# Cross attention and a routed feed-forward layer on one core: the hidden blocks of four tiles are written one place sooner in SyncE's queue, and the first vector steps change places

## The chip, the cores and the metric

The kernel runs on one core of one Trainium2 chip. The metric is the device time of one execution in microseconds (us), the median of several runs. The kernel before: 429.78 us, the median of 3 runs (424.73, 433.81 and 429.78).

## What is computed

The reference, cut to what matters. `x` is (8, 512, 512), 4096 rows of 512; the context is (8, 120, 512); there are 8 experts, each with two 512x512 matrices.

```python
x = x + xattn(k=ctx, v=ctx, q=layernorm(x), Wk, Wq, Wv, bv, bq, Wo, bo)   # softmax attention, one head
xf = layernorm(x).reshape(-1, 512)
idx = argmax(softmax(xf @ Wg + bg))                    # one expert for each row
h = gelu(xf @ W1[e] + b1[e])                           # exact gelu
y = h @ W2[e] + b2[e]
out = x + y[the row's expert]
```

## The kernel before

**Stages.** Up to about 95 us the weights are prepared and products that don't depend on `x` are made. Then 32 tiles of 128 rows go through the attention (about 95 to 205 us). Each row is normalised, its expert is picked, and GpSimd scatters it with an indirect transfer into a DRAM area `routed`, where every expert has its own span. Then the feed-forward part runs over NJ = 39 tiles of 128 routed rows, numbered 0 to 38, each with one expert.

**One tile t of the feed-forward part**, with the helpers that do it:

1. SyncE's queue loads the rows twice: `load_blocks(t)` (line 565, four transfers, as column blocks for the turn) and `load_rows(t)` (line 548, for the residual).
2. VectorE's `x2_turn(t)` (line 1220) transposes 32x32 blocks; ScalarE's `x2_high(t)` (line 946) and VectorE's `x2_low(t)` (line 1225) split the result into two float16 parts.
3. TensorE's `up(t)`: 12 matmuls (lines 1626 and 1629), the up-product, with results in one of two banks. It waits for `x2_low(t)` and for the copy of tile t-2.
4. ScalarE's `copy_hidden(t)` (line 954) copies the product out of the bank. SyncE's `write_hidden(t)` (line 575) writes it to a DRAM block, one for even and one for odd tiles, and `load_hidden(t)` (line 583) reads it back as column blocks, once the write has landed.
5. VectorE's `h_turn(t)` (line 1301) turns it, ScalarE's `gelu(t)` (line 960) and `g_high(t)` (line 968) and VectorE's `g_low(t)` (line 1306) follow.
6. TensorE's `down(t)`: for the first eight tiles one matmul that spreads the bias (line 1617) and then 12 matmuls. The bias matmul waits for `finish(t-2)`, which frees the bank, and the 12 wait for `g_low(t)`.
7. GpSimd's `residual(t)` (line 766, with 774 for tiles from 8 on) prepares the residual, VectorE's `finish(t)` (line 1312) adds the product, and GpSimd's `send(t)` (line 780) scatters the rows to the output.

**Order on TensorE around the change**: up 0, up 1, up 2, up 3, up 4, down 0, the count of the tiles, down 1, and from there up t followed by down t-3: up 5, down 2, up 6, down 3, up 7, down 4, up 8, down 5, up 9 and so on. Between them stand eight single matmuls that spread biases (line 1617 too).

**Tables.** Which rows and which expert a tile has stands in a table. Its first eight columns (NE = 8) are made early from the first rows counted. The other 31 come from lines 1345 to 1372 on VectorE (the *late table*), after all rows are counted, and each reader waits for it. SyncE then loads first rows into registers (line 539, one load of so many values).

**Queues.** Every engine works through its own list in order, and a waiting instruction holds up all behind it. On SyncE `step(t)` runs in the order `write_hidden(t)`, `load_blocks(t+4)`, `load_rows(t+3)`, `load_hidden(t)`. Exceptions at the start: `load_blocks(5)` follows `load_hidden(0)`. In step 5 (`NE - 3`) the order is `write_hidden(5)`, `load_hidden(5)`, the wait for the late table and all scattered rows, one load of seven values, `load_blocks(8)`, `load_blocks(9)`, `load_rows(8)`. On VectorE `step(t)` runs `finish(t-4)`, `g_low(t-2)`, `h_turn(t-1)`, `x2_low(t+2)`, `x2_turn(t+3)`, with the first of these written out by hand. GpSimd scatters the last four row tiles (line 743), then makes the residuals 0 to 2.

## Time and profile before

| | value |
|---|---|
| runs shown | 424.73, 433.81, 429.78 us, median 429.78 |
| the profiled execution | 431.77 us, of which the span from first to last instruction is 430.0 us |
| busy in the span | TensorE 397.0 us, VectorE 321.3, GpSimd 261.1, ScalarE 251.1 |

How to read it: busy time is an average over stages. TensorE is busy for 92% of the span, so time can only come out of its pauses and out of stretches in which it runs at half its clock. In the rows below, the timeline has the start in us, the duration in us, the engine, the line, the operation, what it writes and reads, how many instructions are merged, and in brackets how long the engine had stood idle and what ended that.

### The profile page before, as it was taken

To read this page: it belongs to the slowest core of one execution; us is meant where nothing else is said; L and a number is where in the kernel's file an instruction comes from. 1 tells how busy PE (TensorE), PEld (TensorE's weight loads), DVE (VectorE), ACT (ScalarE), POOL (GpSimd) and SP (SyncE) were. 2 spreads that over 40 slices of the span, in tenths; PEclk is the share of its full clock that TensorE was granted. 3 is DMA by queue.
4 is the path that set the end of the run, shared out by engine and by line. 5 is a ranking of instruction groups with operands and counts; after the bars stand their busy time and mean duration, and the time that the engine had idled before them with its cause. 6 is when DMAs were issued, how large, how long until landed. Compare 5 with 4: busy or idle time off the path is not lost.

```text
span 430.0 us, 8879 instructions
## 1 busy us (share of the span) xinstructions
PE 397.0 (92%) x2097; PEld 219.8 (51%) x2097; DVE 321.3 (75%) x658; ACT 251.1 (58%) x571; POOL 261.1 (61%) x338
## 2 busy tenths in 40 slices
PE   7999999979999998978879799999999999999980
PEld 4657774648777676653334244444444444444430
DVE  4399939994688788887787587778868896988640
ACT  5351128668888887855565365555555555656530
POOL 6089861409457877676783347668546776576730
PEclk9999999999999999998999899999999999999996
DMA  8998999908345596464895887988798979898510
GB/s 274 375 390 297 341 423 416 361 6 319 99 164 176 159 329 183 154 206 129 258 279 164 225 247 235 254 238 225 228 267 249 264 247 258 233 270 240 182 51 0
DMA packets 77984, 101.19 MB, mean 235 GB/s; under 512 B 9075, under 2 KB 49023, under 8 KB 76152
## 3 DMA queue, kind: packets, MB, share of 16 engines
q1 hardware_dynamic: 69664, 80.74, 61.1%
q0 software_dynamic: 6400, 19.65, 12.4%
q10 hardware_dynamic: 1880, 0.31, 0.4%
q8 instruction: 19, 0.31, 0.3%
q14 instruction: 21, 0.17, 0.1%
HBM read 70.80 MB, written 31.28 MB: 237 GB/s over the span
## 4 chain that ended last, share of the span: by engine, by line
PE 41%; DMA 19%; DVE 11%; SPq 11%; issue 9%; POOL 5%; ACT 2%; DVEq 0%; ACTq 0%; POOLq 0%
PE bank L1626 9%; DMA hidden_blocks<-work 7%; DMA work<-hidden_blocks 6%; SPq L565 5%; PE bank L1533 5%; PE bank L1629 5%; PE bank L1468 5%; POOL routed_rows L743 3%; DMA hidden_blocks<-keys_values_then_rows_b 3%; PE bank L1409 3%; PE bank L1488 2%; DMA routed_rows<-work,slot_index 2%; PE bank L1564 2%; PE bank L1580 2%; PE bank L1448 2%
## 5 line engine op out<-in xcount | busy, mean ns | idle before, releaser
L780 POOL DMA_INDIRECT out_x<-keys_values_then_rows_b x39 | 42.5, 1089 | 62.9 <-DVE keys_values_then_rows_b L1312 57.3
L1626 PE MATMUL bank<-expert_weights 128*128 x312 | 75.4, 385 | 4.5 <-DVE expert_weights L1225 2.8
L1626 PE MATMUL bank<-expert_weights,ey_bias_split_then_geluT 128*128 x312 | 74.7, 383 | 3.7 <-DVE ey_bias_split_then_geluT L1306 3.7
L960 ACT ACTIVATE work<-work,b_columns 128x128 f32<-128x128 f32 x144 | 46.0, 390 | 20.6 <-DVE work L1301 15.6
L1301 DVE STREAM_TRANSPOSE work<-work 128x512 f32<-128x512 f32 x36 | 41.4, 1150 | 20.5 <-DMA work<-hidden_blocks 20.4
L1626 PEld LDWEIGHTS bank<-expert_weights 128*128 128x128 f16 x312 | 30.8, 99 | 44.0 <-issue 12.2
L954 ACT ACTIVATE work<-bank 128x512 f32<-128x512 f32 x36 | 21.5, 596 | 53.6 <-PE bank L1629 53.5
L1626 PEld LDWEIGHTS bank<-expert_weights,ey_bias_split_then_geluT 128*128 128x128 f16 x312 | 30.6, 98 | 41.1 <-issue 7.5
L774 POOL TENSOR_TENSOR keys_values_then_rows_b<-keys_values_then_rows_b 128x512 f32<-128x512 f32 x31 | 43.1, 1390 | 7.7 <-POOL keys_values_then_rows_b L766 7.5
L743 POOL DMA_INDIRECT routed_rows<-work,slot_index x32 | 33.1, 1035 | 23.6 <-DVE slot_index L1169 15.6
L1629 PE MATMUL bank<-expert_weights,ey_bias_split_then_geluT 128*128 x156 | 40.8, 385 | 0.0
L766 POOL TENSOR_SCALAR keys_values_then_rows_b<-keys_values_then_rows_b 128x512 f32<-128x512 f32 x39 | 35.8, 920 | 8.0 <-ACT keys_values_then_rows_b L974 6.2
L1629 PE MATMUL bank<-expert_weights 128*128 x156 | 40.2, 380 | 0.0
L1306 DVE TENSOR_TENSOR ey_bias_split_then_geluT<-work,ey_bias_split_then_geluT 128x512 f16<-128x512 f32 x36 | 26.8, 743 | 13.3 <-ACT ey_bias_split_then_geluT L968 13.1
L825 ACT ACTIVATE expert_weights<-expert_weights 128x512 f16<-128x512 f32 x52 | 31.7, 625 | 8.2 <-DVE expert_weights L1082 8.1
L1082 DVE SCALAR_TENSOR_TENSOR expert_weights<-expert_weights 128x512 f16<-128x512 f32 x52 | 34.8, 700 | 1.4 <-ACT expert_weights L825 0.4
L1580 PE MATMUL bank<-keys_values_then_rows_b,work 120*128 120x512 f32 x64 | 35.3, 634 | 0.0
L1564 PE MATMUL bank<-keys_values_then_rows_b,work 128*128 128x128 f32 x256 | 33.8, 275 | 0.0
L1225 DVE TENSOR_TENSOR expert_weights<-key_bias_then_xn,expert_weights 128x512 f16<-128x512 f32 x39 | 32.3, 829 | 1.4 <-ACT expert_weights L946 1.4
L1564 PEld LDWEIGHTS bank<-keys_values_then_rows_b,work 128*128 128x128 f32 x256 | 31.1, 192 | 0.6 <-ACT work L891 0.6
L946 ACT ACTIVATE expert_weights<-key_bias_then_xn 128x512 f16<-128x512 f32 x39 | 24.2, 619 | 11.4 <-DVE key_bias_then_xn L1220 11.1
L1312 DVE SCALAR_TENSOR_TENSOR keys_values_then_rows_b<-bank,keys_values_then_rows_b 128x512 f32<-128x512 f32 x39 | 25.6, 656 | 4.3 <-PE bank L1629 4.2
(214 smaller groups left out, 749.3 us busy)
## 6 DMA issues: line engine op xcount, KB each, us to landing
expert_weights<-in_L_ffn_W SPq DMA_DIRECT2D x14, 1024.0 KB, 14.4
keys_values_then_rows_b<-routed_rows SPq DMA_DIRECT2D x39, 258.0 KB, 3.6
hidden_blocks<-work SPq DMA_DIRECT2D x36, 256.0 KB, 3.8
work<-hidden_blocks SPq DMA_DIRECT2D x36, 256.0 KB, 3.4
expert_weights<-in_x SPq DMA_DIRECT2D x16, 512.0 KB, 4.8
expert_weights<-in_x SPq DMA_DIRECT2D x24, 256.0 KB, 3.2
work<-routed_rows SPq DMA_DIRECT2D x72, 64.0 KB
key_bias_then_xn<-routed_rows SPq DMA_DIRECT2D x68, 64.0 KB, 2.7
```

Source lines behind the costliest of these rows:

```text
L743: pool.indirect_dma_start(routed, bass.IndirectOffsetOnAxis(ap=slot_i[:, j:j + 1], axis=0), rows[:, j, :], None).then_inc(sent[j], 16)
L766: x1_again = nc.gpsimd.tensor_scalar(row[:, 0:D], row[:, 0:D], row[:, D + 3:D + 4], row[:, D:D + 1], ALU.mult, ALU.add)
L774: nc.gpsimd.tensor_tensor(row[:, 0:D], row[:, 0:D], kv[:, bass.ds(ex + b2_at, D)], ALU.add).then_inc(res_ready, 1)
L780: pool.indirect_dma_start(out_rows, ids_of, rrow[t.buf][:, 0:D], None, bounds_check=T - 1, oob_is_err=False).then_inc(out_sent[t.buf], 16)
L960: nc.scalar.activation(hid_turned_of(t)[:, P * c:P * (c + 1)], hid_turned_of(t)[:, P * c:P * (c + 1)], ACT.Gelu, bias=b1_cols[:, :, :].rea ...
L1082: nc.vector.scalar_tensor_tensor(w_split[:, bass.ds(n * 2 * D + D, D)], wall[:, bass.ds((n + GAP) * D, D)], WSCALE, w_split[:, bass.ds(n * ...
L1225: nc.vector.tensor_tensor(x2T[t.half][:, C:2 * C, :], xn2_turned.rearrange("p (c t) -> p c t", c=C), x2T[t.half][:, 0:C, :], ALU.subtract) ...
L1301: nc.vector.transpose(hid_turned_of(t).rearrange("p (c j a) -> p a c j", c=C, a=C), hid_in_of(t).rearrange("p (a i c) -> p a c i", a=C, c= ...
L1564: mm(bank[2 + j % 2][:, 0:P], xnT[j % 2][:, c, :], kv[:, bass.ds(b * (2 * D) + c * P, P)], start=(c == 0), stop=False)
L1580: mm(bank[6 + j % 2][:, :], probT[j % 2], kv[0:K, bass.ds(b * (2 * D) + D, D)], start=True, stop=True)\
L1626: mm(o, a[:, c, :], w_split[:, bass.ds(first + (2 * c + h) * D, D)], start=(c == 0 and h == 0 and not begun), stop=False)
L1629: last = mm(o, a[:, C + c, :], w_split[:, bass.ds(first + 2 * c * D, D)], start=False, stop=(c == C - 1))
```

## The change

On SyncE:

- `write_hidden(1)` to `write_hidden(4)` move ahead in the queue: 1 stands behind `load_hidden(0)` and ahead of `load_blocks(5)`; 2 ahead of `load_hidden(1)`; 3 ahead of `load_hidden(2)`; 4 ahead of `load_hidden(3)`, which now also stands ahead of `load_blocks(7)` and `load_rows(6)`.
- Each `write_hidden` outside the loop waits besides until the block's earlier contents were read (`hl_in`): tile 2 for `load_hidden(0)`, 3 for 1, 4 for 2, and so on.
- In step 5 the late table is read in two parts: one value, `load_blocks(8)`, then `load_hidden(5)`, then six values, then `load_blocks(9)`.

On ScalarE `copy_hidden(3)` goes ahead of `gelu(0)`, and `copy_hidden(4)` ahead of `gelu(1)`. On VectorE `h_turn(1)` goes ahead of `g_low(0)`; `finish(0)`, `g_low(2)`, `h_turn(3)` and `finish(1)` go ahead of the late table, `g_low(3)` into it ahead of its first comparison; `h_turn(4)` and `x2_low(7)` follow `x2_turn(7)`; and `x2_turn(8)` goes behind `finish(2)` and `g_low(4)`. On GpSimd `residual(0)` and `residual(1)` go ahead of the wait for the last picks. No product, copy, turn or byte moved by a transfer is added or taken away.

```diff
             def write_hidden(t):
                 wait_apart(sp, hc_done, t.j + 1, sp_waits)
+                if isinstance(t.j, int):
+                    need(sp, hl_in[t.half], 16 * t.pair)
                 sp.dma_start(hidden[...], hid_of(t)...).then_inc(hw_in[t.half], 16)
...
             def step(t):
-                if t.real:
+                if t.real and not (isinstance(t.j, int) and 0 < t.j <= C):
                     write_hidden(t)
+                if isinstance(t.j, int) and t.j == C - 1:
+                    write_hidden(t + 1)
+                    load_hidden(t)
                 if isinstance(t.j, int) and t.j == NE - 3:
+                    late_ready()
+                    starts.update(enumerate(first_rows(NE, 1), NE))
+                    load_blocks(t + 3, starts[(t + 3).base])
                     load_hidden(t)
-                    late_ready()
-                    starts.update(enumerate(first_rows(NE, FIRST + 4 - NE), NE))
-                    load_blocks(t + 3, starts[(t + 3).base])
+                    starts.update(enumerate(first_rows(NE + 1, FIRST + 3 - NE), NE + 1))
...
+                if isinstance(t.j, int) and t.j in (1, C - 2):
+                    write_hidden(t + 1)
-                if t.real and not (isinstance(t.j, int) and t.j == NE - 3):
+                if t.real and not (isinstance(t.j, int) and t.j in (C - 1, NE - 3)):
                     load_hidden(t)
                 if isinstance(t.j, int) and t.j == 0:
+                    write_hidden(Slot(1))
                     load_blocks(Slot(C + 1), starts[C + 1])
...
# GpSimd, scale()
                 if n == 2 * NTURN - 1:
+                    residual(Slot(0))
+                    residual(Slot(1))
                     pool.wait_ge(picked, n + 1)
...
-            for n in range(3):
-                residual(Slot(n))
+            residual(Slot(2))
...
# ScalarE
-                if t.real:
+                if t.real and not (isinstance(t.j, int) and t.j <= C):
                     copy_hidden(t)
...
+            copy_hidden(Slot(3))
             gelu(Slot(0))
             g_high(Slot(0))
+            copy_hidden(Slot(4))
...
# VectorE
             pick_experts(c, 2 * NTURN - 1, 1)
+            h_turn(Slot(1))
             g_low(Slot(0))
-            h_turn(Slot(1))
             place(c, 2 * NTURN - 1, 1)
...
             h_turn(Slot(2))
+            finish(Slot(0))
             x2_low(Slot(5))
             x2_turn(Slot(6))
+            g_low(Slot(2))
+            h_turn(Slot(3))
+            finish(Slot(1))

             dve.wait_ge(counted, 1)
...
-            g_low(Slot(2))
-            finish(Slot(0))
             x2_low(Slot(6))
+            g_low(Slot(3))
...
-            h_turn(Slot(3))
...
             x2_turn(Slot(7))
+            h_turn(Slot(4))
+            x2_low(Slot(7))
...
                 if (t - 2).real:
                     g_low(t - 2)
+                if isinstance(t.j, int) and t.j == NE - 2:
+                    x2_turn(t + 2)
...
-            each_step(dve, step, 5, NJ + 4)
+            each_step(dve, step, NE - 2, NJ + 4)
```

## Rows read from the trace of the kernel before

**Rows 1.** Windows: stretch, PE, PEld, DVE, ACT, POOL busy, clock, DMA share, GB/s

```profile
242.00:244.00 2.00, 2.00 (x6) 0.69 (x5) 1.87 (x3) 1.97 (x6) 1.17 (x1) 0.50 1.10 297
262.00:320.00 58.00, 57.84 (x268) 26.09 (x267) 45.81 (x54) 33.01 (x77) 37.85 (x34) 1.00 0.85 246
```

**Rows 2.** Waits, 205 to 246 us: total us, times, longest

```profile
PE bank L1617 <- DVE keys_values_then_rows_b L1312: 4.3, 2, 2.5
```

**Rows 3.** Timeline of TensorE, down 1 to up 9

```profile
218.43 1.90 PE L1626 MATMUL bank<-expert_weights,ey_bias_split_then_geluT 128*128 x8 [1.11 <-DVE ey_bias_split_then_geluT L1306]
...
226.11 0.39 PE L1617 MATMUL bank<-b_split,expert_rows_one_hot 104*128 104x512 f16 x1 [1.86 <-DVE keys_values_then_rows_b L1312]
...
240.21 0.39 PE L1617 MATMUL bank<-b_split,expert_rows_one_hot 104*128 104x512 f16 x1 [2.47 <-DVE keys_values_then_rows_b L1312]
240.81 2.89 PE L1626 MATMUL bank<-expert_weights,ey_bias_split_then_geluT 128*128 x8 [0.22 <-DVE ey_bias_split_then_geluT L1306]
...
245.09 1.89 PE L1626 MATMUL bank<-expert_weights 128*128 x8
...
251.15 1.89 PE L1626 MATMUL bank<-expert_weights 128*128 x8
```

**Rows 4.** Timeline of SyncE's queue, tiles 1 to 9 of the feed-forward part

```profile
206.78 0.46 SPq L575 DMA_DIRECT2D hidden_blocks<-keys_values_then_rows_b  x1
...
211.52 0.34 SPq L583 DMA_DIRECT2D keys_values_then_rows_b<-hidden_blocks  x1
...
219.94 0.41 SPq L583 DMA_DIRECT2D keys_values_then_rows_b<-hidden_blocks  x1
220.41 0.45 SPq L575 DMA_DIRECT2D hidden_blocks<-work  x1
...
232.59 0.32 SPq L583 DMA_DIRECT2D keys_values_then_rows_b<-hidden_blocks  x1
235.02 1.89 SPq L565 DMA_DIRECT2D work<-routed_rows  x4
...
239.43 0.42 SPq L575 DMA_DIRECT2D hidden_blocks<-work  x1
...
242.77 0.35 SPq L583 DMA_DIRECT2D work<-hidden_blocks  x1
```

**Rows 5.** Issue to landing of the hidden blocks 184 to 262 us: line 575, then line 583

```profile
DMA to landing us min/median/max: 3.1/3.9/6.8
...
DMA to landing us min/median/max: 2.8/3.6/5.9
```

**Rows 6.** Table loads of 7 values and of 1

```profile
L539 SPq TENSOR_LOAD <-tile_table x1: 1625/1625/1625, 233.2 to 233.2; - x1
...
L539 SPq TENSOR_LOAD <-tile_table x1: 280/280/280, 392.8 to 392.8; - x1
```

**Rows 7.** Timeline of VectorE, 209 to 249 us

```profile
213.18 1.00 DVE L1306 TENSOR_TENSOR ey_bias_split_then_geluT<-work,ey_bias_split_then_geluT 128x512 f16<-128x512 f32 x1 [1.16 <-ACT ey_bias_split_then_geluT L968]
...
221.98 0.13 DVE L1345 SCALAR_TENSOR_TENSOR tiles_int<-bank,expert_base_rows 128x8 int32<-128x8 f32 x1
...
229.39 0.33 DVE L1369 TENSOR_SCALAR tile_table<-late_table_by_column 1x31 int32<-1x31 f32 x3
...
238.41 1.08 DVE L1220 STREAM_TRANSPOSE key_bias_then_xn<-work 128x512 f32<-128x512 f32 x1 [4.63 <-DMA work<-routed_rows]
...
247.25 1.13 DVE L1301 STREAM_TRANSPOSE work<-work 128x512 f32<-128x512 f32 x1 [2.31 <-DMA work<-hidden_blocks]
248.27 0.65 DVE L1225 TENSOR_TENSOR expert_weights<-key_bias_then_xn,expert_weights 128x512 f16<-128x512 f32 x1
```

**Rows 8.** Timeline of ScalarE, copy 3

```profile
213.05 0.58 ACT L954 ACTIVATE keys_values_then_rows_b<-bank 128x512 f32<-128x512 f32 x1
```

**Rows 9.** Timeline of GpSimd at the wait for the last picks

```profile
212.12 3.45 POOL L735 TENSOR_SCALAR work<-work,neg_mean_x 128x512 f32<-128x512 f32 x4 [2.03 <-DVE expert_one_hot L1154]
```

**Rows 10.** Line 766 on GpSimd, 222.5 to 225 us: ns min/median/max

```profile
L766 POOL TENSOR_SCALAR keys_values_then_rows_b<-keys_values_then_rows_b x4: 761/797/1225, 222.5 to 224.8; 128x512 f32<-128x512 f32 x4
```

## The prediction

> **What bounds the kernel now.** I read first the busy time by windows, then TensorE's waits, then the timelines of TensorE, SyncE's queue and VectorE side by side. From 262 to 320 us TensorE is busy for 57.84 of 58 us at full clock [rows 1]; the reader is to see that in the steady part nothing but TensorE's own work counts, and that a start made earlier by some us brings the end forward by as much, if the rest keeps up. What can be won lies between the first down-products and up 9. There TensorE waited 4.3 us in two places for `finish`, which frees the bank of the down-product [rows 2]. In order of time [rows 3]: 1.11 us at down 1, 1.86 at the bias matmul of down 2, 2.47 and 0.22 at down 4. Then down 4 ran at half clock (0.50, its level of 1.2 GHz [rows 1]): its 12 matmuls take from 240.81 to 245.09, 4.3 us, where a product takes 2.6 (up 9 of rows 3 stands 6.06 after up 8, which is two products, 5.2, and the bias matmuls between). That costs 1.7. Together 1.11 + 1.86 + 2.47 + 0.22 + 1.7 = 7.4 us.
>
> What stands behind the 2.47 us is on VectorE: `x2_turn(8)` waited 4.63 us for its column blocks, with `finish(2)` and `g_low(4)` behind it [rows 7]. Its transfers left SyncE's queue only at 235.02, while the late table was ready at 229.7 (229.39 + 0.33) [rows 4, 7]: the queue stood at `load_hidden(5)`, issued at 232.59, and then loaded seven values in 1.62 us [rows 4, 6].
>
> **SyncE, the writes.** No transfer is added. `write_hidden(1)`, 206.78 before, no longer has the four transfers of `load_blocks(5)` ahead (four take 1.89 us [rows 4]): 204.8. Tile 2's write follows about 208.3 (after the four block transfers, a row load and the landing of `load_hidden(0)`), `load_hidden(1)` about 209.5 instead of 211.52. `copy_hidden(3)`, 213.05 before, loses `gelu(0)` and `g_high(0)` ahead of it and comes as soon as up 3 is done, about 2 us sooner [rows 8]. Tile 3's write waits (new) for `load_hidden(1)`: 209.5 + 3.6 [rows 5], 213. `load_hidden(2)` leaves at 213.4 and lands at 217.0, and the second new wait, that of `write_hidden(4)`, is over only then. Queued behind that wait are `load_hidden(3)`, `load_blocks(7)`, two row loads and `load_hidden(4)`. Still `write_hidden(4)` leaves at 217.1 instead of 220.41 and `load_hidden(3)` at 217.5 instead of 219.94 [rows 4]. From there landings are slow, since the last four scatters are on the DMA engines: the longest write took 6.8 us and the longest read 5.9, where the medians are 3.9 and 3.6 [rows 5]. For `load_hidden(3)` the bounds are 2.8 and 5.9 (6.8 if it fares like the write); I take 5.9, since that is what this very transfer is the likeliest to meet: landed at 223.4.
>
> **VectorE.** `h_turn(1)` ahead of `g_low(0)` waits for `load_hidden(1)`, about 213, and takes 1.1, so `g_low(0)`, which ran at 213.18 [rows 7], starts about 0.4 later, and down 0 with it: cost 0.4. `gelu(1)` starts sooner for it, and down 1 comes at 217.6 with 0.1 us of waiting instead of 1.11. Down 2's bias matmul no longer waits, as `finish(0)` comes ahead of the table's work, and down 2 is over at 226.1. But `h_turn(3)` now stands ahead of the table, and waits for `load_hidden(3)` until 223.4. From the first table instruction to the last the work before took 229.72 - 221.98 = 7.7 us [rows 7], with a turn, a `finish`, an `x2_low` and a `g_low` among it. The new order from `h_turn(3)` on has the same four and the same table work, so the table is ready at 223.4 + 7.7 = 231.1, 1.4 later than before. Halfway, 4.9 after `h_turn(3)` begins (7.7 less the half of the table, 2.1, and a `g_low`, 0.7: my estimate), `x2_low(6)` is done at 228.3, and TensorE waits for it at up 6: 228.3 - 226.1 = 2.2 us. That is what is late next.
>
> **SyncE, the table.** One value takes 0.28 us and seven 1.62 [rows 6], so six take about 1.40 ((1.62 - 0.28) / 6 = 0.22 each): one and six together cost the same as seven, plus some 0.3 us around a load. `load_blocks(8)` leaves at 231.1 + 0.28 + 0.5 = 231.9, 3.1 sooner than 235.02. Then come `load_hidden(5)`, 233.8 (1.2 later than 232.59, hidden: its turn stands behind `x2_turn(8)` and down 5 isn't due before 243), six values and `load_blocks(9)` and `load_rows(8)`: `write_hidden(6)` leaves at about 238.8 instead of 239.43; the queue sets this, not tile 6's copy, which is ready some us before. `load_hidden(6)` leaves at 242.1 instead of 242.77.
>
> **TensorE at up 9.** `finish(2)` and `g_low(4)` no longer stand behind `x2_turn(8)`: down 4 starts at about 237 without a long wait, 3.7 sooner, and at full clock. Up 8 follows at 240 and down 5 is over at 246.3. Up 9 needs `x2_low(9)`, which VectorE does behind `h_turn(6)`. Before, `h_turn(6)` waited 2.31 us for `load_hidden(6)`, and `x2_low(9)` ended at 248.92 [rows 7], 2.2 us ahead of up 9 at 251.15 [rows 3]. Now it ends 0.7 sooner, 248.2, and up 9 waits 1.9 us for it. The sum: 7.4 removed, 0.4 + 0.1 + 2.2 + 1.9 = 4.6 new, net 2.8 us; the direct reading agrees, up 9 at 248.3 instead of 251.15. From there TensorE has nothing but its own work again, since `write_hidden` and `load_hidden` need less than its 5.2 us a tile (0.4, four block transfers 1.9, 0.4, 0.35 and the rest of a landing).
>
> **GpSimd.** `residual(0)` and `residual(1)` fill the 2.03 us that it waited for the last picks [rows 9]; two take 2 x 0.8 = 1.6 us, and 2.4 at the slow end of line 766 [rows 10]. If the cover were gone the scatters would go 0.4 later. I cost it at nothing. In rows 10 the same instruction takes 761 ns and 1225 ns, so something beside it holds it up. The Trainium skill (SBUF — State Buffer, Who interferes with whom) says that VectorE instructions with two SBUF inputs and GpSimd instructions that read SBUF lock each other out for a whole instruction. By that rule VectorE's picks, which now run beside a residual, could lose up to one residual; the sum would then be 2.0 and not 2.8.
>
> **The time.** The profiled execution took 431.77 us with a span of 430.0. 430.0 - 2.8 = 427.2, execution 429.0, a ratio of 0.9935; on the median of 429.78 that is 427.0.
>
> **Rivals.**
> (a) *Forecast*: 427.0, with 426 to 428.5 as its own range. For it: `load_hidden(6)` hangs on the queue behind the table, which moves little.
> (b) *The gain is given back at up 6 and up 9.* The waits of 2.2 and 1.9 us are about as long as the 2.47 us after which the clock fell before. If it falls at one, 1.7 us go; at both, 3.4. Against: after the 1.86 us at down 2 it didn't fall. Time 428.7 to 430.4.
> (c) *Landings at their fast end.* If `load_hidden(3)` and those before it take 2.8 to 3.1 us [rows 5], each hand-over moves up: `load_hidden(3)` lands at 217.6, `h_turn(3)` then waits only for VectorE's own order and starts at 220.6, the table is ready at 228.3, `load_hidden(6)` leaves at 239, up 9 starts at 244. Net 7.2, time 422.6. For: the writes leave ahead of the scatters. Against: `load_hidden(3)` doesn't. The Trainium skill (DMA: Bandwidth & Descriptors, Anatomy of one DMA) gives about 2 us fixed plus bytes over 436 GB/s, an estimate of 2.6 us for these 256 KB, and by that this rival would hold; the trace has 2.8 as its shortest, 5.9 and 6.8 as its longest.
> (d) *Slower: the new wait of `write_hidden(4)` dams the queue.* Place: step 3 of SyncE. If `load_hidden(2)` lands at 219 and `load_hidden(3)` at 227, the table comes at 234.7, and up 9, 17.2 us behind the table (248.3 - 231.1), at 251.9: time 430.5; with both at 6.8 us after queueing, 432. It decides from a landing of `load_hidden(3)` at 226.2, 2.8 later than I take.
> (e) *The change does nothing*, as the medians hide it: the three runs differ by 9 us.
>
> **Chances.** (a) 0.42, (b) 0.25, (c) 0.18, (d) 0.15; (e) lies within the first two. The prediction is (a), 427.0. The range of 421.5 to 431.5 takes in (c) with 1 us beyond, and (d) up to 431.5; it is as wide as this since the runs themselves spread by 4 to 5 us about their median. 2% of 429.78 is 8.6 us, about what a measurement here can tell from no change: only (c) with a median of luckier runs reaches below 421.2, 0.08, and only (d) with unlucky ones above 438.4, 0.04. Within 2%: 0.88.
>
> **What the profile after would show.** Right: no wait of TensorE for line 1312; down 4 at clock 1.00; `x2_turn(8)` behind line 1306 with less than 1 us of waiting; a wait of about 2 us for line 1225 at up 6 and at up 9; late table at 231; `load_blocks(8)` 3 us sooner. Wrong: line 583 of tile 3 landed by 221 or after 226, the clock at 0.50 after either wait, or new waits for line 1306 in the steady part, which would mean that the chain through SyncE doesn't keep up.

## The result, and the profile after

The changed kernel takes 432.25 us (median of 20 runs, 428.03 to 438.28), the kernel before 430.15 us (20 runs, 424.73 to 435.68): ratio 1.0068, 95% interval 1.0046 to 1.009. On another chip the ratio was 1.0129 (1.0078 to 1.018). A ratio is taken over the runs within 1.5% of their kernel's fastest, so it isn't quite the quotient of the medians. The change makes the kernel slower by 0.7 to 1.3%, 3 to 5.5 us.

Two traces were taken of each kernel. Three marks of TensorE's timeline cut them: the start of up 4, the start of up 9 and the end of the span. The last column is the sum of TensorE's waits for `x2_low` from 255 to 400 us.

| trace | span | up 4 starts | up 4 to up 9 | up 9 to the end | waits for `x2_low`, 255 to 400 us |
|---|---|---|---|---|---|
| before | 430.0 | 210.27 | 40.9 | 178.9 | 0.6 |
| before, second | 422.9 | 206.56 | 38.4 | 178.0 | 0.2 |
| after | 431.6 | 208.50 | 40.5 | 182.6 | 3.4 |
| after, second | 432.2 | 209.85 | 39.1 | 183.3 | 4.3 |

Up to up 9 the two kernels are alike (39.6 us on average before, 39.8 after). The loss stands behind it: 4.5 us, from 178.4 to 182.9 on average, in a part whose code was not touched. By TensorE's busy time in that part (165.0 and 164.6 us before, 165.9 twice after), about 3.5 of the 4.5 us are idle time and about 1 is longer busy time, which no run explains.

TensorE's timeline of the changed kernel, the lines that answer to [rows 3] (columns as there; up and down are lines 1644 and 1647, `g_low` is 1318, `x2_low` 1237, `h_turn` 1313, `x2_turn` 1232, `finish` 1324):

```profile
216.19 3.59 PE L1644 MATMUL bank<-expert_weights,ey_bias_split_then_geluT 128*128 x8 [4.59 <-DVE ey_bias_split_then_geluT L1318]
...
221.28 0.21 PE L1723 MATMUL bank<-picks_seen,ones_f 128*128 128x8 f16 x1
...
249.01 1.90 PE L1644 MATMUL bank<-expert_weights 128*128 x8 [1.06 <-DVE expert_weights L1237]
...
266.22 1.90 PE L1644 MATMUL bank<-expert_weights 128*128 x8 [1.03 <-DVE expert_weights L1237]
...
277.25 1.90 PE L1644 MATMUL bank<-expert_weights 128*128 x8 [0.50 <-DVE expert_weights L1237]
...
288.28 1.90 PE L1644 MATMUL bank<-expert_weights 128*128 x8 [0.50 <-DVE expert_weights L1237]
```

The waits for `finish` of [rows 2] are gone, as forecast. In their place, down 0 waited 4.59 us for `g_low(0)` and then took 5.1 us (216.19 to 221.28) where a product takes 2.6. And there are waits for `x2_low` in the steady part, at a distance of 11.03 us from each other, which is two tiles. The windows of the changed kernel answer to [rows 1]: half clock at down 0, and in the steady part TensorE busy 55.38 of 58 us instead of 57.84 (a few records are missing from either):

```profile
218.00:220.00 2.00, 2.00 (x6) 0.63 (x5) 1.54 (x2) 0.92 (x3) 1.39 (x3) 0.50 0.56 189
...
262.00:320.00 58.00, 55.38 (x254) 24.74 (x253) 47.45 (x52) 31.92 (x73) 36.84 (x33) 1.00 0.82 239
```

SyncE's queue of the changed kernel (line 577 writes a hidden block, 585 loads it; compare [rows 4]), and what ended the waits on ScalarE and VectorE:

```profile
204.67 0.45 SPq L577 DMA_DIRECT2D hidden_blocks<-keys_values_then_rows_b  x1
...
210.15 0.34 SPq L585 DMA_DIRECT2D keys_values_then_rows_b<-hidden_blocks  x1
...
218.70 0.51 SPq L585 DMA_DIRECT2D keys_values_then_rows_b<-hidden_blocks  x1
...
233.73 1.87 SPq L565 DMA_DIRECT2D work<-routed_rows  x4
...
240.02 0.40 SPq L577 DMA_DIRECT2D hidden_blocks<-work  x1
...
243.27 0.35 SPq L585 DMA_DIRECT2D work<-hidden_blocks  x1
```

```profile
210.16 0.60 ACT L964 ACTIVATE keys_values_then_rows_b<-bank 128x512 f32<-128x512 f32 x1 [2.72 <-DMA hidden_blocks<-keys_values_then_rows_b]
211.11 1.28 ACT L970 ACTIVATE work<-work,b_columns 128x128 f32<-128x128 f32 x4 [0.35 <-issue]
...
227.20 0.60 ACT L964 ACTIVATE keys_values_then_rows_b<-bank 128x512 f32<-128x512 f32 x1 [2.44 <-PE bank L1647]
227.69 1.08 ACT L984 ACTIVATE keys_values_then_rows_b<-bank 128x512 f32<-128x512 f32 x2
228.65 1.28 ACT L970 ACTIVATE keys_values_then_rows_b<-keys_values_then_rows_b,b_columns 128x128 f32<-128x128 f32 x4
```

```profile
214.39 1.13 DVE L1313 STREAM_TRANSPOSE keys_values_then_rows_b<-keys_values_then_rows_b 128x512 f32<-128x512 f32 x1 [3.58 <-DMA keys_values_then_rows_b<-hidden_blocks]
215.39 0.66 DVE L1318 TENSOR_TENSOR ey_bias_split_then_geluT<-work,ey_bias_split_then_geluT 128x512 f16<-128x512 f32 x1
...
230.62 0.69 DVE L1318 TENSOR_TENSOR ey_bias_split_then_geluT<-keys_values_then_rows_b,ey_bias_split_then_geluT 128x512 f16<-128x512 f32 x1 [2.16 <-ACT ey_bias_split_then_geluT L978]
...
232.91 0.33 DVE L1383 TENSOR_SCALAR tile_table<-late_table_by_column 1x31 int32<-1x31 f32 x3
```

The reader is to see three things. Write 1 left at 204.67, 2.1 us sooner than in [rows 4], but was in DRAM only at 210.1, after 5.4 us, and its reading, issued at 210.15, landed at 214.4, after 4.2 us. `h_turn(1)` stood idle 3.58 us for it, with `g_low(0)` behind it, whose input had been ready since 213.0: down 0 waited for a turn that it doesn't need. And the late table was ready at 233.2, since `g_low(3)`, now in the middle of it, waited 2.16 us for `gelu(3)` and `g_high(3)` (line 978). The turn was not what it lacked: `h_turn(3)` had ended at 225.8. But on ScalarE `gelu(3)` (228.65) stands behind `copy_hidden(5)` (227.20) and two copies of biases (line 984), and `copy_hidden(5)` had waited 2.44 us for up 5, which came late by what down 0 had lost. In the same way `copy_hidden(3)`, put ahead of `gelu(0)`, waited 2.72 us for write 1 to land (210.16), and `gelu(0)` began at 211.11, 1.2 us behind the end of `h_turn(0)` (209.87), where it had been 0.1 before.

### The profile page after: what moved, and what is told of

Its sections match the earlier page's. It is cut to its first block, busy times and chain, and to the rows that moved or that the text cites. A ratio compares the mean times of both kernels' runs of the same rounds, so it can differ in the third digit from the quotient of the medians.

```text
span 431.6 us, 8893 instructions
## 1 busy us (share of the span) xinstructions
PE 397.3 (92%) x2097; PEld 219.1 (51%) x2097; DVE 323.1 (75%) x658; ACT 251.9 (58%) x571; POOL 260.4 (60%) x338
## 4 chain that ended last, share of the span: by engine, by line
PE 45%; DMA 14%; issue 12%; DVE 11%; SPq 8%; POOL 4%; ACT 3%; another core or an unknown queue 0%; ACTq 0%; POOLq 0%; DVEq 0%
PE bank L1644 10%; DMA work<-hidden_blocks 6%; PE bank L1551 5%; PE bank L1647 5%; PE bank L1486 5%; SPq L565 5%; PE bank L1582 4%; PE bank L1427 3%; PE bank L1598 3%; PE bank L1506 2%; DMA hidden_blocks<-work 2%; PE bank L1574 2%; DVE expert_weights L1237 2%; POOL routed_rows L754 2%; DMA routed_rows<-work,slot_index 2%
## 5 line engine op out<-in xcount | busy, mean ns | idle before, releaser
L791 POOL DMA_INDIRECT out_x<-keys_values_then_rows_b x39 | 40.7, 1043 | 66.2 <-DVE keys_values_then_rows_b L1324 59.5
L1644 PE MATMUL bank<-expert_weights 128*128 x312 | 73.9, 379 | 6.9 <-DVE expert_weights L1237 5.7
L777 POOL TENSOR_SCALAR keys_values_then_rows_b<-keys_values_then_rows_b 128x512 f32<-128x512 f32 x39 | 37.7, 970 | 7.9 <-ACT keys_values_then_rows_b L984 6.1
L1647 PE MATMUL bank<-expert_weights,ey_bias_split_then_geluT 128*128 x156 | 40.9, 386 | 0.0
L1647 PE MATMUL bank<-expert_weights 128*128 x156 | 40.0, 379 | 0.0
L1237 DVE TENSOR_TENSOR expert_weights<-key_bias_then_xn,expert_weights 128x512 f16<-128x512 f32 x39 | 35.2, 902 | 1.4 <-issue 0.7
```

What stands on the lines that cost most here:

```text
L777: x1_again = nc.gpsimd.tensor_scalar(row[:, 0:D], row[:, 0:D], row[:, D + 3:D + 4], row[:, D:D + 1], ALU.mult, ALU.add)
L791: pool.indirect_dma_start(out_rows, ids_of, rrow[t.buf][:, 0:D], None, bounds_check=T - 1, oob_is_err=False).then_inc(out_sent[t.buf], 16)
L1237: nc.vector.tensor_tensor(x2T[t.half][:, C:2 * C, :], xn2_turned.rearrange("p (c t) -> p c t", c=C), x2T[t.half][:, 0:C, :], ALU.subtract) ...
L1644: mm(o, a[:, c, :], w_split[:, bass.ds(first + (2 * c + h) * D, D)], start=(c == 0 and h == 0 and not begun), stop=False)
L1647: last = mm(o, a[:, C + c, :], w_split[:, bass.ds(first + 2 * c * D, D)], start=False, stop=(c == C - 1))
```

## The experiments

Two theories at the start. T1: the loss is down 0 (the wait and the half clock). T2: it arises behind up 9. Each kernel below is timed against the kernel before on its own chip; ratios carry a 95% interval. "Gap" is up 4 to up 9 and "rest" is up 9 to the end, in us, from one trace.

**e1: `g_low(0)` first.** The changed kernel with one pair put back.

```diff
             pick_experts(c, 2 * NTURN - 1, 1)
-            h_turn(Slot(1))
             g_low(Slot(0))
+            h_turn(Slot(1))
```

> The changed kernel with one line of VectorE's list put back: g_low(0) ahead of h_turn(1). Theory T1 (the loss comes from down 0, which waited 4.59 us behind h_turn(1) and then ran at half clock, 2.5 us): down 0 waits about 1 us as before and runs at clock 1.00, up 9 starts 3 to 6 us sooner after up 4 than the 40.5 us of the changed kernel, and the time is 3 us or more below the changed kernel's, ratio to before 0.99 to 1.00. Theory T2 (the loss arises behind up 9, in the steady part: 182.6 us from up 9 to the end against 178.9 before): what is won ahead of up 9 does not reach the end, the stretch from up 9 to the end stays at 182 us or grows, ratio to before 1.004 to 1.01.

Measured: ratio 1.0012 (0.9974 to 1.005), 428.35 us. Gap 37.9, rest 181.3; the wait at down 0 is 2.00 us and the half clock is still there, where T1 expected 1 us and full clock (`copy_hidden(3)` holds `gelu(0)` back by 1.1 us in this trace too), and TensorE waits 1.37 us at 262.53 for `x2_low`. Against the changed kernel's 1.0068 and 1.0129 the one pair is worth 2.4 to 5 us, from ratios on different chips whose intervals allow 0.5 to 7.8; its gap is 1.9 us shorter than the changed kernel's average. But what the front wins over before (39.6 to 37.9) is given back in the rest (178.4 to 181.3). Both theories have a part.

**e2, e3, e4: one side of the change at a time.** e2 is the kernel before with the new SyncE and ScalarE, e3 with the new VectorE and GpSimd, e4 with the table in two parts and `x2_turn(8)` moved, nothing else:

```diff
                 if isinstance(t.j, int) and t.j == NE - 3:
+                    late_ready()
+                    starts.update(enumerate(first_rows(NE, 1), NE))
+                    load_blocks(t + 3, starts[(t + 3).base])
                     load_hidden(t)
-                    late_ready()
-                    starts.update(enumerate(first_rows(NE, FIRST + 4 - NE), NE))
-                    load_blocks(t + 3, starts[(t + 3).base])
+                    starts.update(enumerate(first_rows(NE + 1, FIRST + 3 - NE), NE + 1))
...
                     g_low(t - 2)
+                if isinstance(t.j, int) and t.j == NE - 2:
+                    x2_turn(t + 2)
...
-                if (t + 3).real:
+                if (t + 3).real and not (isinstance(t.j, int) and t.j == NE - 3):
                     x2_turn(t + 3)
```

> The kernel before with the new order of SyncE's queue and ScalarE's two copies, VectorE and GpSimd as before. T1: down 0 as before (wait about 1 us), so no loss; the writes come 2 to 3 us sooner but finish and x2_turn(8) still stand where they did; ratio 0.99 to 1.00. T2, if the queue's new phase makes the steady part slow: up 9 to the end 182 us instead of 178.9, ratio 1.004 to 1.01.

> The kernel before with VectorE's and GpSimd's new order, SyncE and ScalarE as before. h_turn(1) ahead of g_low(0) now waits for load_hidden(1) at its old place (landed about 214.3), so down 0 waits at least as long as in the changed kernel, 4.5 us or more. T1: slower than the changed kernel or equal to it, ratio to before 1.005 to 1.015, all of the loss standing ahead of up 9. T2: the stretch from up 9 to the end is 182 us in spite of SyncE's old order if VectorE's order is what changes the steady part, 179 if it is the queue's.

> The kernel before with two things only: the table read in two parts with load_blocks(8) ahead of load_hidden(5), and x2_turn(8) behind finish(2) and g_low(4). The prediction's reading of the 2.47 us at down 4: that wait and the half clock behind it (1.7 us) go, up 9 starts up to 2.2 us sooner. T1: this reaches the end, ratio 0.993 to 0.998. T2: up 9 to the end grows by as much, ratio 0.998 to 1.005.

Measured: e2 1.001 (0.9969 to 1.0051), e3 1.0028 (0.9992 to 1.0064), e4 0.9999 (0.996 to 1.0037). Gap and rest: e2 37.5 and 181.5; e3 40.1 and 179.7; e4 39.9 and 181.0. In e4 no wait of TensorE at down 4 is left. None of the three is measurably faster or slower than before, so e3 misses the 1.005 to 1.015 that T1 gave it. Each of the traces has waits for `x2_low` in the rest (2 to 4 us), which the two traces of before have not: either any of the moves calls them up, or two traces of before don't show all that it does. In e3 down 0 waited 4.54 us, with SyncE's old order: the long wait at down 0 comes with VectorE's order. But e2, with VectorE's old order, waited 2.52 us there, 0.9 more than the 1.65 of the second trace of before: in e2 `copy_hidden(3)` waited 1.78 us for write 1, with `gelu(0)` behind it.

**Before and after again.** No edit.

> The kernel before once more, one look, for a second trace. Where up 9 comes about 40.9 us behind up 4, the stretch from up 9 to the end is expected at 179 us with under 3 us of waits, as in the first trace. If it comes out at 181 or more, the first trace of before was lucky there and the comparison of the two steady parts from single traces doesn't hold.

> The changed kernel once more, for its ratio on the same chip as the next two and a second trace. Expected of both theories: ratio to before about 1.007, down 0 waits over 4 us and starts at half clock. T1 (h_turn(1) ahead of g_low(0) is the loss) expects it 2 to 3 us above the kernel with that line put back. If the trace's stretch from up 9 to the end is again about 182 us, the steady part is slower whenever up 9 is not late; if it is 179, the first trace had bad luck there.

Measured: the rest is 178.0 in the second trace of before and 183.3 in the second of after (ratio 1.0129), so in two traces of each the steady part is slower in the changed kernel. The second trace of before shows something else, in the same places as [rows 3]:

```profile
223.96 0.39 PE L1617 MATMUL bank<-b_split,expert_rows_one_hot 104*128 104x512 f16 x1 [1.75 <-DVE keys_values_then_rows_b L1312]
236.27 1.90 PE L1626 MATMUL bank<-expert_weights,ey_bias_split_then_geluT 128*128 x8 [0.21 <-DVE ey_bias_split_then_geluT L1306]
```

```profile
222.00:240.00 18.00, 15.95 (x73) 7.07 (x73) 15.36 (x32) 11.54 (x26) 8.14 (x8) 1.00 0.79 224
```

The wait of 2.47 us at down 4 and the half clock behind it are not there: 0.21 us, and a clock of 1.00. The traces of e7 and e12 (below), whose order is that of the kernel before up to down 4, haven't them either (no wait, and some 0.3 us), so they were a matter of one execution in four. A stretch at half clock is there all the same, at down 0, behind a wait of 1.65 us:

```profile
213.00:215.00 2.00, 2.00 (x6) 0.76 (x5) 1.79 (x6) 1.51 (x5) 0.97 (x3) 0.50 0.93 214
```

**What makes the steady part slow.** The chain of one round in the changed kernel: VectorE, SyncE, what SyncE's queue waited for from 255 to 400 us (line 78 is the helper in which it waits; total us, times, longest), and the instruction of GpSimd (line 785, the second of a residual) that ran beside the first `x2_low`:

```profile
263.19 1.15 DVE L1313 STREAM_TRANSPOSE work<-work 128x512 f32<-128x512 f32 x1 [2.45 <-DMA work<-hidden_blocks]
264.22 1.75 DVE L1237 TENSOR_TENSOR expert_weights<-key_bias_then_xn,expert_weights 128x512 f16<-128x512 f32 x1
266.11 1.10 DVE L1232 STREAM_TRANSPOSE key_bias_then_xn<-key_bias_then_xn 128x512 f32<-128x512 f32 x1
...
274.66 1.16 DVE L1313 STREAM_TRANSPOSE work<-work 128x512 f32<-128x512 f32 x1 [1.56 <-DMA work<-hidden_blocks]
275.70 1.30 DVE L1237 TENSOR_TENSOR expert_weights<-key_bias_then_xn,expert_weights 128x512 f16<-128x512 f32 x1
277.14 1.11 DVE L1232 STREAM_TRANSPOSE key_bias_then_xn<-key_bias_then_xn 128x512 f32<-128x512 f32 x1
```

```profile
267.44 1.86 SPq L565 DMA_DIRECT2D key_bias_then_xn<-routed_rows  x4
270.00 0.31 SPq L548 DMA_DIRECT2D keys_values_then_rows_b<-routed_rows  x1
270.69 0.35 SPq L585 DMA_DIRECT2D work<-hidden_blocks  x1
...
SPq L78 <- DVE key_bias_then_xn L1232: 18.1, 16, 2.1
```

```profile
264.15 1.27 POOL L785 TENSOR_TENSOR keys_values_then_rows_b<-keys_values_then_rows_b 128x512 f32<-128x512 f32 x1 [0.28 <-POOL keys_values_then_rows_b L777]
```

Read as one chain: `h_turn` starts at 263.19 as its block lands; `x2_low` behind it takes 1.75 us and frees up 12, which starts at 266.22 after a wait of 1.03; `x2_turn` ends at 267.2; that frees `load_blocks` on SyncE (267.44), behind which stand `load_rows` (270.00) and `load_hidden` (270.69); it lands at 274.6, and `h_turn` starts at 274.66. The way round is 11.5 us here and 10.9 the next time (`h_turn` at 285.56), TensorE's wait comes back at 277.25 and 288.28 (11.03), and two tiles of TensorE's work are 10.4 (four products of 2.6). It is a ring over two tiles with more in it, in these rounds, than TensorE's own time; from 290 to 400 us only two more waits follow, at 304.70 and 347.47, so it isn't too long in every round. Theory R says that this ring limits, L that GpSimd lengthens `x2_low` in it, P that an uneven start keeps it going, S1 that it is enough to take `x2_low` out of its shadow.

**e12: one delay in the kernel before.**

```diff
+                if isinstance(t.j, int) and t.j == NE - 1:
+                    for _ in range(14):
+                        link(nc.vector.memset(early_v[:, :], 0.0))
                 if (t - 1).real:
                     h_turn(t - 1)
```

> The kernel before with 14 small memsets in a chain on VectorE, some 2.5 to 3 us, once, ahead of h_turn(6). Theory P (one uneven start persists: in the changed kernels h_turn(6) stood idle 2.4 to 3.4 us and the waits for x2_low behind up 9 sum to 2.3 to 4.3 us): waits for x2_low up at up 9 and again every second tile up to about 300 us, 2 us or more behind up 9, time 1 to 3 us above before. If the pipeline forgets it, TensorE waits once at up 9, 1 us or less, and never again; ratio 1.000 to 1.003.

Measured: ratio 1.0032 (1.0002 to 1.0062), rest 180.6. The delay, and TensorE's waits from 255 to 400 us (total, times, longest), first of e12 and then of before for comparison:

```profile
243.29 2.83 DVE L1380 MEMSET early_table_scratch<- 128x80 f32 x14
...
PE bank L1629 <- DVE expert_weights L1225: 2.4, 5, 0.6
```

```profile
PE bank L1626 <- DVE expert_weights L1225: 0.6, 1, 0.6
```

TensorE lost some 0.3 us at up 9, yet five waits came later, the first at 275.28 and the next 11.03 behind it. That agrees with P, in one trace and with a ratio just clear of 1, but doesn't show it. The delay itself is smaller than the chain of 2.83 us, since VectorE stood idle at the same place in both traces of before (2.31 us [rows 7] and 1.37): `load_hidden(6)` left at 240.72, and with the 4.2 to 4.5 us that it took in these two it would have let `h_turn(6)` start at 244.9 to 245.2, not 246.16, an estimate of about 1 us.

What the delay changed can be read at up 9:

```profile
247.19 0.65 DVE L1225 TENSOR_TENSOR expert_weights<-key_bias_then_xn,expert_weights 128x512 f16<-128x512 f32 x1
...
248.09 1.90 PE L1629 MATMUL bank<-expert_weights 128*128 x8
```

Up 9 started 0.25 us behind the end of `x2_low(9)`, as soon as it could: in the changed kernel, where it waited, it is 0.24. Twelve traces have `h_turn` ahead of `x2_low` in the steps: in ten it is 0.24 or 0.25, and in the two of before `x2_low(9)` was ready 2.2 and 1.4 us ahead of up 9. So before enters the steady part with a reserve, and the others without one. That fits the waits that follow; that it causes them was not tested by itself.

**e13 and e14: what is in the ring.** e13 is the changed kernel with `load_rows(t+3)` behind `load_hidden(t)` from step 6 on. e14 is the changed kernel, and e9 is e1, each without the second instruction of a residual (line 785) for tiles from 8 on, so that the expert's bias is missing from their output.

```diff
-                if (t + 3).real and not (isinstance(t.j, int) and t.j < -1):
+                late = not isinstance(t.j, int) or t.j >= NE - 2
+                if (t + 3).real and not late and not (isinstance(t.j, int) and t.j < -1):
                     load_rows(t + 3, starts[(t + 3).base])
...
                     load_hidden(t)
+                if (t + 3).real and late:
+                    load_rows(t + 3, starts[(t + 3).base])
```

> The changed kernel with load_rows(t+3) behind load_hidden(t) in SyncE's steps from 6 on, so that one issue of 0.35 us and the gap before it leave the way from x2_turn through load_blocks to load_hidden. Theory R (a ring of two tiles: load_hidden lands, h_turn, x2_low, x2_turn, load_blocks, load_rows, load_hidden; 11.03 us a round in the changed kernel where TensorE needs 10.4): the round shortens by 0.35 to 0.8 us, TensorE's waits for x2_low behind 255 us fall from 3.4 and 4.3 us to under 2, ratio to before 1.000 to 1.006 instead of 1.0068 and 1.0129. If the queue is no part of the ring (only the hidden block's own round through DRAM counts), waits and time stay.

> The changed kernel without GpSimd's second instruction of a residual (the expert's bias is not added for tiles from 8 on, so that part of the output is left out). Theory L (GpSimd's instruction lengthens x2_low, which feeds the ring): x2_low's mean falls from 988 and 904 ns to 750 or less, TensorE's waits for it from 3.4 and 4.3 us to 1 to 2, the time by 2 to 4 us, ratio to before 0.995 to 1.003. If only the uneven start counts, x2_low gets short and the waits stay at 3 us or more.

> The changed kernel with g_low(0) first, without GpSimd's second instruction of a residual (the expert's bias is not added for tiles from 8 on, so that part of the output is left out). Theory L (GpSimd's residuals hold x2_low up: it takes up to 1.75 us instead of 0.65): x2_low falls to 0.65 to 0.8 us each, TensorE's waits for it in the steady part shrink by half or more, and the time falls by 1 to 3 us. If x2_low gets short and the waits stay, they come from the hidden block's landing alone.

Measured: e13 1.0063 (1.001 to 1.0117), rest 181.0; e14 0.9981 (0.994 to 1.0021), rest 179.4; e9 0.9918 (0.9881 to 0.9956), rest 178.0. TensorE's waits from 255 to 400 us, of after, e13 and e14:

```profile
PE bank L1644 <- DVE expert_weights L1237: 3.4, 5, 1.0
```

```profile
PE bank L1647 <- DVE expert_weights L1240: 1.3, 3, 0.5
```

```profile
PE bank L1637 <- DVE expert_weights L1230: 1.0, 3, 0.6
```

`x2_low` from 250 to 400 us (28 or 29 times; busy us and mean ns), of before, after and e14:

```profile
L1225 DVE TENSOR_TENSOR expert_weights<-key_bias_then_xn,expert_weights 128x512 f16<-128x512 f32 x28 | 24.1, 862 | 0.0
```

```profile
L1237 DVE TENSOR_TENSOR expert_weights<-key_bias_then_xn,expert_weights 128x512 f16<-128x512 f32 x28 | 27.7, 988 | 0.0
```

```profile
L1230 DVE TENSOR_TENSOR expert_weights<-key_bias_then_xn,expert_weights 128x512 f16<-128x512 f32 x29 | 20.9, 721 | 0.0
```

Without GpSimd's instruction `x2_low` takes 721 ns instead of 988 and the waits for it fall from 3.4 to 1.0 us (in e9 740 ns, and 1.2 us instead of e1's 2.5): L holds. The mean alone doesn't tell the kernels apart, though: e4 has 3.6 us of waits with a mean of 863 ns, before 0.6 with 862. By the rule of the Trainium skill (SBUF — State Buffer, Who interferes with whom) `x2_low`, with two SBUF inputs, and GpSimd's instructions that read SBUF hold each other up for a whole instruction; the trace agrees: the `x2_low` of 264.22 took 1.75 us instead of 0.65 and ended at 265.97, 0.55 behind the end of the instruction of line 785 (264.15 + 1.27); at 275.70 and 286.59 it is 0.55 us again. For R the trace of e13 speaks (1.3 us of waits for `x2_low` and 0.4 without a releaser, under the 2 expected); its time doesn't decide, since the interval holds the changed kernel's 1.0068 as well as what R expected.

**e6, e7, e11: `x2_low` ahead of the turn.** The same edit on e1, on before and on the changed kernel, for every step:

```diff
-                if (t - 1).real:
-                    h_turn(t - 1)
                 if (t + 2).real:
                     x2_low(t + 2)
+                if (t - 1).real:
+                    h_turn(t - 1)
```

> The changed kernel with g_low(0) first, and besides, in each of VectorE's steps, x2_low(t+2) ahead of h_turn(t-1). Theory S1 (the steady part gives the gain back because x2_low stands behind an h_turn that waits for its hidden block): TensorE's waits for x2_low between 250 and 300 us (1.37 us at tile 12 in the kernel with g_low(0) first) go, up 9 to the end falls from 181.3 to about 178, ratio to before 0.990 to 0.995. Theory S2 (the chain write, read, turn, gelu, down is itself too long, so a wait only changes its name): TensorE waits as long for line g_low instead, and the time stays at 0.999.

> The kernel before with one thing only: in VectorE's steps x2_low(t+2) ahead of h_turn(t-1). Two traces of before have only 0.6 and 0.2 us of waiting for x2_low behind up 9, so if the order of the first tiles is worth what e6 showed over before, this one stays at 0.995 to 1.000, above e6 (0.990). If x2_low ahead of the turn is the whole of e6's gain, it comes out at 0.990 as well, and the change's own moves are worth nothing.

> The changed kernel (h_turn(1) still ahead of g_low(0)) with x2_low(t+2) ahead of h_turn(t-1) in VectorE's steps. If the loss has two terms, the one at down 0 stays (a wait of over 4 us and half clock) and the one in the steady part goes: up 9 to the end 177 to 178 us instead of 182.6 and 183.3, time 3 to 5 us below the changed kernel, ratio to before 0.997 to 1.002, and 2 to 3 us above e6. If the steady part stays slow, x2_low's place is not its cause.

Measured: e6 0.9899 (0.9846 to 0.9953), gap 36.1, rest 177.0; e7 0.992 (0.9882 to 0.9958), gap 40.6, rest 178.2; e11 0.9938 (0.9907 to 0.9968), gap 37.5, rest 177.0. No wait for `x2_low` is named behind 255 us in any of them (e7 has one wait of 0.98 us without a releaser). The window of e6 that answers to [rows 1]:

```profile
262.00:320.00 58.00, 58.00 (x271) 26.25 (x270) 43.97 (x57) 33.70 (x79) 38.95 (x35) 1.00 0.87 249
```

On the changed kernel the edit is worth 5.9 us of the rest by the traces (182.9 to 177.0), and its ratio falls from 1.0068 and 1.0129 to 0.9938: S1 holds, for the edit as a whole. It does two things at once, though: in its three kernels `x2_low` stands ahead of the wait for the hidden block, and it also takes only 722, 719 and 724 ns on average from 250 to 400 us (e6, e7, e11), as little as in e14, since it now runs at another time than GpSimd's instruction. By single traces the shorter `x2_low` alone (e14) brings the rest from 182.9 to 179.4, and the edit to 177.0. These three beat the kernel before by 0.6 to 1.0%, and the changed kernel by more. Among themselves they can't be told apart (e11, expected at 0.997 to 1.002, came out better), so the change's own moves (e7 has none of them, e11 all) are worth nothing that can be measured even where the steady part doesn't eat them. e11 keeps its 3.54 us of waiting at down 0 and isn't measurably slower than e7; against e6, from which it differs by the pair of e1 alone, it is 0.4% slower, 1.7 us, within the intervals.

**e10: `x2_turn` ahead of the turn too.** e6 with the last two of each step exchanged.

```diff
                 if (t + 2).real:
                     x2_low(t + 2)
-                if (t - 1).real:
-                    h_turn(t - 1)
                 if (t + 3).real:
                     x2_turn(t + 3)
+                if (t - 1).real:
+                    h_turn(t - 1)
```

> e6 with x2_turn(t+3) ahead of h_turn(t-1) too, so that SyncE's load_blocks, which waits for x2_turn, no longer hangs on the landing of a hidden block. If the loop of two tiles (load_hidden, h_turn, x2_turn, load_blocks, load_hidden) still limits anything in e6, the time falls 1 us or more, 0.986 to 0.989. If e6 is at TensorE's own rate from up 9 on (its stretch to the end was 177.0 us with 2 us of waits, all in the tail), it stays at 0.990, or rises by 1 us since the turn comes 1.1 us later and gelu with it.

Measured: ratio 1.0449 (1.04 to 1.0498), 448.79 us. I had expected 1 us at most either way from e6; it is 19 us above before, and some 23 above e6 by the ratios. VectorE's round, and what TensorE waited for from 255 to 400 us:

```profile
294.71 1.00 DVE L1318 TENSOR_TENSOR ey_bias_split_then_geluT<-work,ey_bias_split_then_geluT 128x512 f16<-128x512 f32 x1 [1.55 <-issue]
295.63 0.68 DVE L1237 TENSOR_TENSOR expert_weights<-key_bias_then_xn,expert_weights 128x512 f16<-128x512 f32 x1
296.45 1.11 DVE L1232 STREAM_TRANSPOSE key_bias_then_xn<-key_bias_then_xn 128x512 f32<-128x512 f32 x1
297.49 1.09 DVE L1313 STREAM_TRANSPOSE work<-work 128x512 f32<-128x512 f32 x1
...
PE bank L1644 <- DVE ey_bias_split_then_geluT L1318: 13.0, 22, 0.7
```

Here a ring of one tile closes: `g_low` 294.71, `x2_low`, `x2_turn`, `h_turn` to 298.6, then on ScalarE `gelu` (1.28) and `g_high` (0.63), and the next `g_low` at 300.68: 5.97 us a tile against TensorE's 5.2. In e6 `x2_turn`'s 1.1 us are outside this ring, and it needs 4.9 (an estimate, 5.97 less 1.1).

## Why the prediction was wrong

1. **"Together ... 7.4 us" can be won.** The sum of pauses was taken from one execution. Its largest term, 2.47 + 1.7 us at down 4, was absent from the second trace of before (0.21 us, clock 1.00) and from e7 and e12. Of the terms only the wait at down 2 stands in all four traces with this order (1.86, 1.75, 1.91 and 1.91 us); the 1.11 us at down 1 were 0, 1.00 and 0.21 in the other three, and the half clock was elsewhere. e4, which takes just the wait at down 4 away, measures 0.9999.
2. **"down 0 with it: cost 0.4".** `g_low(0)` came at 215.39 instead of 213.18, 2.2 us later. I took 3.9 and 3.6 us for the landings of write and read of tile 1, the medians of [rows 5], where 5.4 and 4.2 came. Besides, TensorE was 1.8 us earlier at that point than in the trace of before (up 4 at 208.50 instead of 210.27, which no edit brought), so the same lateness was a longer wait: 4.59 us. I had priced half clock at up 6 and up 9, but not here, where it fell: 2.5 us (5.1 less 2.6). That part isn't the change's alone, since the second trace of before, e7 and e12 have half clock at down 0 too. In the first pair of traces this step took 3.6 + 2.5 = 6.1 us instead of 0.4, which with 1.06 us at up 9 used up nearly all of the 7.4: up 4 to up 9 is 0.4 us shorter, not 2.8. `copy_hidden(3)` failed beside it: it was to come "as soon as up 3 is done", but waited 2.72 us for write 1, with `gelu(0)` behind it. e1 puts the pair at 2.4 to 5 us, with wide intervals.
3. **"the table is ready at 231.1".** It was ready at 233.2. `h_turn(3)` began at 224.68, 1.3 us later than worked out, and `g_low(3)` waited 2.16 us in the table's middle, not for `h_turn(3)` (done at 225.8) but for ScalarE, where `gelu(3)` stood behind `copy_hidden(5)`, late by down 0. The equality of the content was right, the waits inside it were left out. `load_blocks(8)` left at 233.73 instead of 231.9, `load_hidden(6)` at 243.27 instead of 242.1, and up 9 started at 249.01 instead of 248.3.
4. **The new waits at up 6 and up 9.** At up 6 none: `x2_low(6)` ended at 228.5, as worked out (228.3), but TensorE, held up at down 0, came only at 230.46. At up 9 1.06 instead of 1.9 us.
5. **"From there TensorE has nothing but its own work again."** This is the step that cost the sign. The argument compared SyncE's issues for one tile with 5.2 us and never followed a chain that comes back to itself. The ring of two tiles takes 10.9 to 11.5 us in the first rounds of the changed kernel, where TensorE needs 10.4, and TensorE waits for `x2_low` for 3.4 and 4.3 us in all (255 to 400 us). The part behind up 9 is 4.5 us longer, more than the whole front was to bring: with the front alone missed the time would have stayed about where it was, and e11, which takes these waits away, is faster than before. The prediction did name the sign of it ("new waits ... in the steady part"), though it looked for them on line `g_low`, and it gave them no rival and no chance.
6. **Rival (c)** takes its sum from the Trainium skill (DMA: Bandwidth & Descriptors, Anatomy of one DMA), which gives it for transfers that GpSimd issues; SyncE issues these, and the two that mattered took 5.4 and 4.2 us, not the 2.6 of the sum. **Rival (b)** had against it that the clock didn't fall after 1.86 us at down 2; in e7 and e12 it did, after 1.91 us.
7. **Right**: the waits for `finish` went; SyncE's `load_blocks(8)` came sooner; `residual(0)` and `residual(1)` cost nothing on GpSimd; a slower outcome by rival (d)'s mechanism didn't occur, `load_hidden(3)` left at 218.70 and `h_turn(3)` started at 224.68.

What stays open: why the kernel before, alone among the orders tried without e6's edit, runs its steady part without the waits in its two traces. The reserve at up 9 (2.2 and 1.4 us) tells it from the others and P fits it, but neither was tested alone. It is also open whether the two traces stand for the kernel: e7 takes these waits away and gains 0.8% on before, though they had next to none to take (0.6 and 0.2 us). The spread of each kernel's runs (424.73 to 435.68 for before) was not explained either.

## What to carry to other kernels

Before a gain ahead of a long steady part is counted, close the rings in it: follow each chain through every in-order queue until it comes back to its own start, add it up with the waits at their usual length, and compare with the bound engine's time for as many tiles. In an in-order list put what the bound engine needs next ahead of whatever waits for a transfer (`x2_low` ahead of `h_turn`, `g_low(0)` ahead of `h_turn(1)`), but add up the ring that this lengthens: one more turn ahead of `h_turn` made a kernel that had been 1% faster than before 4.5% slower. Look at what a copy moved forward waits for: `copy_hidden(3)` waited for a write to land and held `gelu(0)` back. And take pauses from several traces before calling them winnable: the largest here was in one of four.

## What the runs showed of the hardware that I had not expected

- The same VectorE instruction (`x2_low`, 128x512, two SBUF inputs) took from 0.64 to 1.75 us in one trace, by what GpSimd did beside it; the slow ones ended 0.55 us behind GpSimd's instruction of line 785. Without that instruction the mean fell from 988 to 721 ns, and with `x2_low` one place sooner in VectorE's list to 724 (e11).
- The length of a wait doesn't tell whether TensorE's clock falls. At the same place, down 0, it stood at 0.50 after waits of 1.65 us (second trace of before), 1.82 (e10) and 4.59 us (after), and at 1.00 after waits of 1.54 us (e6) and 2.52 us (e2). At down 2 it stood at 1.00 after 1.86 and 1.75 us (both traces of before) and at 0.50 after 1.91 us (e7 and e12). The kernel before has its stretch at half clock at down 4 in one trace and at down 0 in the other. A term of a sum that counts on its going is uncertain by its whole size, some 2 us.
- A write of 256 KB to DRAM took 5.4 us to land and its reading 4.2 us, at a point where I had taken 3.9 and 3.6 from the medians.
